# Inverse roots of a graph layer's norms: from GpSimd's power to ScalarE's logarithm and exponential with a Newton step on VectorE

## What is computed

```python
def _layernorm(x, axis=-1, eps=1e-05):
    m, v = jnp.mean(x, axis, keepdims=True), jnp.var(x, axis, keepdims=True)
    return (x - m) / jnp.sqrt(v + eps)

def _L1_gnn_ref(inp, adj, W1, W2, W3):                  # inp = layernorm(x)
    h1, h2, h3 = inp @ W1, inp @ W2, inp @ W3
    e = leaky_relu(einsum('bnd,bmd->bnm', h1, h2), 0.2)
    e = where(adj > 0, e, -1e12)
    return relu(softmax(e) @ h3)

def _L1_ffn_ref(x, Wg, bg, ...):                        # x = layernorm(x)
    top_w, top_i = top_k(x @ Wg + bg, 2)                # then 8 experts, two for each token
```

## Time and profile before

| | us |
|---|---|
| median of 3 runs | 1431.46 (1427.86 to 1432.95) |
| the profiled execution, its own time | 1429.35 |
| its span, first to last instruction | 1427.3 |
| second graph layer, about | 870 to 1132 |
| busy: TensorE, VectorE, ScalarE, GpSimd | 1154.3, 991.3, 694.0, 868.2 |

### The profile page before, as it was taken

One profiled execution on the slowest core, in us unless ns is written; L12 is line 12 of the kernel. 1 busy time (PEld: TensorE's weight loads), 2 busy tenths in 40 slices (PEclk: granted clock), 3 DMA queues, 4 the chain that ended last, 5 costly groups with the idle time before them and its releaser, 6 DMA issues. The chain is left out here.

```text
span 1427.3 us, 33176 instructions
## 1 busy us (share of the span) xinstructions
PE 1154.3 (81%) x9205; PEld 957.5 (67%) x9205; DVE 991.3 (69%) x3903; ACT 694.0 (49%) x1789; POOL 868.2 (61%) x754
## 2 busy tenths in 40 slices
PE   6999999667677741999999993787774199999996
PEld 4776666556676641888888882454543199989995
DVE  4999999978787744577767664878775345565555
ACT  5766666457877831333333331333332145455553
POOL 3567676554477676344444441267777568887887
PEclk9999999899999975999999997777676599999999
DMA  6400000000011112566565673244332245555554
GB/s 186 68 2 2 1 2 2 1 1 24 22 37 41 35 49 79 180 198 199 189 203 192 193 220 108 67 139 121 99 116 63 81 57 72 69 66 67 74 67 46
DMA packets 126253, 122.61 MB, mean 86 GB/s; under 512 B 16576, under 2 KB 108096, under 8 KB 126128
## 3 DMA queue, kind: packets, MB, share of 16 engines
q1 hardware_dynamic: 92720, 85.65, 21.4%
q0 software_dynamic: 32960, 35.36, 12.7%
q10 hardware_dynamic: 448, 0.10, 0.0%
HBM read 76.71 MB, written 44.34 MB: 85 GB/s over the span
## 5 line engine op out<-in xcount | busy, mean ns | idle before, releaser
L2851 POOL DMA_INDIRECT out<-m_yb,m_dsti x142 | 227.5, 1602 | 64.3 <-DVE m_yb L2951 27.4
L2151 POOL DMA_INDIRECT rows<-m_yb,m_dsti x135 | 129.2, 957 | 170.1 <-DVE m_dsti L2282 148.5
L2227 ACT ACTIVATE m_sg<-psum 128x256 f32<-128x256 f32 (+3 forms) x216 | 79.6, 369 | 179.5 <-PE psum L2180 175.5
L1375 POOL DMA_INDIRECT dispatch<-g_flat,g1r_pos x128 | 129.5, 1012 | 51.6 <-issue 32.7
L1117 POOL DMA_INDIRECT dispatch<-common_v,a1r_pos x128 | 125.0, 976 | 52.9 <-issue 35.7
L2180 PE MATMUL psum<-m_xT,m_w 128*128 128x256 f32 (+3 forms) x648 | 140.3, 366 | 0.6 <-ACT m_xT L2218 0.6
L2924 ACT ACTIVATE m_hT<-psum,m_w 128x256 f32<-128x256 f32 (+1 forms) x240 | 92.6, 446 | 98.6 <-PE psum L2878 97.7
L2180 PEld LDWEIGHTS psum<-m_xT,m_w 128*128 128x128 f32 (+1 forms) x648 | 106.2, 178 | 18.3 <-ACT m_xT L2218 1.0
L2889 PE MATMUL psum<-m_w,m_hT 128*128 128x128 f32 x848 | 104.8, 275 | 1.1 <-ACT m_hT L2924 0.6
L2878 PE MATMUL psum<-m_xT,m_w 128*128 128x256 f32 (+1 forms) x480 | 104.0, 360 | 1.0 <-issue 0.8
L2889 PEld LDWEIGHTS psum<-m_w,m_hT 128*128 128x128 f32 x848 | 99.4, 192 | 1.8 <-ACT m_hT L2924 1.6
(11 more groups left out here) (313 smaller groups left out, 3068.7 us busy)
## 6 DMA issues: line engine op xcount, KB each, us to landing
m_w<-in_c_wall SPq DMA_DIRECT2D x54, 533.0 KB
ahead_w<-in_c_wall SPq DMA_DIRECT2D x18, 533.0 KB, 3.5
g1c_y<-rows SPq DMA_DIRECT2D x32, 256.0 KB, 3.4
m_xg<-dispatch SPq DMA_DIRECT2D x47, 132.0 KB
m_xg<-dispatch SPq DMA_DIRECT2D x46, 130.0 KB, 2.2
resident<-in_c_wall SPq DMA_DIRECT2D x8, 578.0 KB, 6.1
out<-x SPq DMA_DIRECT2D x16, 256.0 KB
out<-m_yb,m_dsti POOLq DMA_INDIRECT x142, 3.3
```

Of the source, the lines that this page charges most:

```text
L1375: pool.indirect_dma_start(out=dest, out_offset=bass.IndirectOffsetOnAxis(ap=self.pos[t % 3][:, k, p:p + 1], axis=0), in_=flat[:, p, :], in ...
L2151: pool.indirect_dma_start(out=rows_out, out_offset=bass.IndirectOffsetOnAxis(ap=dsti[j][:, t:t + 1], axis=0), in_=yb[j][:, t, :], in_offse ...
L2227: act.activation(sg[j % 2][0:cn, k, 0:rows], up_banks[j % 2][k][0:cn, 0:rows], ACT.Silu)\
L2851: pool.indirect_dma_start(out=out_rows, out_offset=bass.IndirectOffsetOnAxis(ap=dsti[j][:, t:t + 1], axis=0), in_=yb[j][:, t, :], in_offse ...
```

## The change

Each root is now formed as exp(-0.5 ln v), by two ACTIVATEs on ScalarE (`guess_root`), and mended by one Newton step r = g (1.5 - 0.5 v g^2), three instructions on VectorE (`root`). An Ln on one column stands ahead of ScalarE's loop. GpSimd's loop is left with the scatters: all of a batch at once, in the step in which its positions are due. The diff, with what is only declarations and signals cut:

```diff
                     act.activation(fT[:, :], bT[:, :], ACT.Copy).then_inc(fT_ready.sem, 1)
 
+                def guess_root(i, k):
+                    if not runs(i):
+                        return
+                    act.wait_ge(*vs[k].now(i))
+                    act.wait_ge(*rs_ready[k].before(i))
+                    act.activation(lv[:, k, :], ve[:, k, :], ACT.Ln).then_inc(ln_ready[k].sem, 1)
+                    act.wait_ge(*ln_ready[k].now(i))
+                    act.activation(guess[:, k, :], lv[:, k, :], ACT.Exp, scale=-0.5).then_inc(guessed[k].sem, 1)
+
+                act.activation(ahead.probe[:, :], h3[:, 0, C:C + 1], ACT.Ln)
+
                 def step(g, b, h):
                     flat_T(g - 1)
                     probs_T(g)
                     mixed_out(g)
                     head_xT(g + 1)
+                    guess_root(g, 1)
                     head(g + 1)
+                    guess_root(g + 2, 0)
                     scores_own(g + 1)
...
+                def root(i, k):
+                    if not runs(i):
+                        return
+                    dve.wait_ge(*guessed[k].now(i))
+                    dve.wait_ge(*(flat_ready if k else xn_ready).before(i))
+                    dve.tensor_tensor(square[:, k, :], guess[:, k, :], guess[:, k, :], ALU.mult).then_inc(newton[k].sem, 1)
+                    dve.wait_ge(*newton[k].now(i, 0))
+                    dve.scalar_tensor_tensor(out=miss[:, k, :], in0=square[:, k, :], scalar=-0.5, in1=ve[:, k, :],
+                                             op0=ALU.mult, op1=ALU.mult).then_inc(newton[k].sem, 1)
+                    dve.wait_ge(*newton[k].now(i, 1))
+                    dve.scalar_tensor_tensor(out=rs[:, k, :], in0=miss[:, k, :], scalar=1.5, in1=guess[:, k, :],
+                                             op0=ALU.add, op1=ALU.mult).then_inc(rs_ready[k].sem, 1)
 
                 def head_xn(i):
                     if not runs(i):
                         return
-                    dve.wait_ge(*rs0_ready.now(i))
+                    dve.wait_ge(*rs_ready[0].now(i))
...
                     if t is not None:
                         R.vector_rows(dve, t, bR)
+                    root(g + 1, 0)
                     head_xn(g + 1)
...
                         R.vector_choose(dve, t, bR)
+                    root(g, 1)
                     flat_norm(g, h)
...
-                    pool.tensor_tensor(rs[:, 0, :], ve[:, 0, :], half[:, 0:PG], ALU.pow).then_inc(rs0_ready.sem, 1)
...
-                    pool.tensor_tensor(rs[:, 1, :], ve[:, 1, :], half[:, 0:PG], ALU.pow).then_inc(rs1_ready.sem, 1)
...
                 def step(g, b, h):
-                    t, u, v = [batch_due(g, lag) for lag in (3, 4, 5)]
-                    last = t is not None and BATCHES[t][1] == PG
-                    if v != LAST_PAIR:
-                        some(v, 13, 16)
-                    some(t, 0, 3)
-                    some(u, 5, 11)
-                    root_flat(g)
-                    some(t, 3, 4)
-                    some(u, 11, 12)
-                    root_head(g + 2)
-                    some(t, 4, 5)
-                    some(u, 12, 13 if u != LAST_PAIR else 16)
-                    if last:
-                        R.pool_scatter(pool, t, 0, 2 * PG, batch_rows(flat, t), dest)
+                    t = batch_due(g, 3)
+                    if t is not None:
+                        R.pool_scatter(pool, t, 0, 2 * BATCHES[t][1], batch_rows(flat, t), dest)
```

More of the change, by code:

```diff
@@ L2363, in phase_gnn1 @@
         ve, rs = sb("ve", [128, 2, PG]), sb("rs", [128, 2, PG])
+        lv, guess = sb("lv", [128, 2, PG]), sb("guess", [128, 2, PG])
+        square, miss = sb("square", [128, 2, PG]), sb("miss", [128, 2, PG])
         xn = sb("xn", [128, PG, C])
@@ L2390, in phase_gnn1 @@
         gate = sig("gate")
-        dve_signals = bn + part + vs + [xn_ready, e_steps, rc_ready, x3_ready, flat_ready]\
+        newton, rs_ready = [sig("newton0", 2), sig("newton1", 2)], [sig("rs0_ready"), sig("rs1_ready")]
+        dve_signals = bn + part + vs + newton + rs_ready + [xn_ready, e_steps, rc_ready, x3_ready, flat_ready]\
             + R.dve_signals + M.dve_signals
@@ L2394, in phase_gnn1 @@
         own_ready = sig("own_ready")
-        act_signals = [xT_ready, h12_ready, h3_ready, own_ready, pt_ready, o_ready, fT_ready] + R.act_signals
-        rs0_ready, rs1_ready = sig("rs0_ready"), sig("rs1_ready")
-        pool_signals = [rs0_ready, rs1_ready] + R.pool_signals
+        ln_ready, guessed = [sig("ln0"), sig("ln1")], [sig("guessed0"), sig("guessed1")]
+        act_signals = ln_ready + guessed + [xT_ready, h12_ready, h3_ready, own_ready, pt_ready, o_ready, fT_ready] + R.act_signals
+        pool_signals = R.pool_signals
         pe_xT, pe_h, pe_e, pe_pt, pe_o, pe_fT = sig("pe_xT"), sig("pe_h", 3), sig("pe_e"), sig("pe_pt"), sig("pe_o", 2), sig("pe_fT")
@@ L2603, in head_stats @@
                     norm_stats(dve, lambda p: xt(i, p), st[:, 0, :, :], mv0[i % 2], ve[:, 0, :], bn[0], part[0],
-                               vs[0], i, EPS_LN, gate, [M.mixed.now(i, 1), rs0_ready.before(i)])
+                               vs[0], i, EPS_LN, gate, [M.mixed.now(i, 1), rs_ready[0].before(i)])
+                def root(i, k):
[10 more added lines that the diff above has]
+                                             op0=ALU.add, op1=ALU.mult).then_inc(rs_ready[k].sem, 1)
                 def head_xn(i):
@@ L2649, in flat_stats @@
                     norm_stats(dve, lambda p: xt(i, p), st[:, 1, :, :], mv1, ve[:, 1, :], bn[1], part[1],
-                               vs[1], i, EPS_LN, gate, [x3_ready.now(i), rs1_ready.before(i)])
+                               vs[1], i, EPS_LN, gate, [x3_ready.now(i), rs_ready[1].before(i)])
                 def flat_norm(i, t):
@@ L2654, in flat_norm @@
                         return
-                    dve.wait_ge(*rs1_ready.now(i))
+                    dve.wait_ge(*rs_ready[1].now(i))
                     R.wait_block(dve, i // 2 - 3)
@@ L2683, in _ @@
             def _(pool):
[L2684 to L2688, removed]
-                    pool.tensor_tensor(rs[:, 0, :], ve[:, 0, :], half[:, 0:PG], ALU.pow).then_inc(rs0_ready.sem, 1)
[L2691 to L2695, removed]
-                    pool.tensor_tensor(rs[:, 1, :], ve[:, 1, :], half[:, 0:PG], ALU.pow).then_inc(rs1_ready.sem, 1)
-                def some(t, first, last):
-                    if t is not None and BATCHES[t][1] == PB:
-                        R.pool_scatter(pool, t, first, last, batch_rows(flat, t), dest)
-                def step(g, b, h):
-                    t, u, v = [batch_due(g, lag) for lag in (3, 4, 5)]
-                    last = t is not None and BATCHES[t][1] == PG
-                    if v != LAST_PAIR:
-                        some(v, 13, 16)
-                    some(t, 0, 3)
-                    some(u, 5, 11)
-                    root_flat(g)
-                    some(t, 3, 4)
-                    some(u, 11, 12)
-                    root_head(g + 2)
-                    some(t, 4, 5)
-                    some(u, 12, 13 if u != LAST_PAIR else 16)
-                    if last:
-                        R.pool_scatter(pool, t, 0, 2 * PG, batch_rows(flat, t), dest)
+                def step(g, b, h):
+                    t = batch_due(g, 3)
+                    if t is not None:
+                        R.pool_scatter(pool, t, 0, 2 * BATCHES[t][1], batch_rows(flat, t), dest)
                 in_pairs(step)
```

## The result

The changed kernel takes 1441.41 us (median of 9 runs, 1435.21 to 1442.57), beside 1430.58 for the kernel before (9 runs, 1423.31 to 1432.95). The ratio is 1.0083, with a 95% interval of 1.0066 to 1.0100: slower by 0.8%, some 12 us (the medians lie 10.8 apart). The profiled execution took 1441.74 us; its span is 1439.9. The prediction was 1440.

The account below looks back on a forecast made before the run. VectorE was taken to bound choosing groups, a chain through TensorE and ScalarE rows groups, with GpSimd's lateness hurting a few. Longer groups and start, less a shorter tail, gave +8.4 us on the layer: 1440, range 1435 to 1452.

Parts of the forecast that it names:

- two table loads a root: On ScalarE Ln and Exp each need a table load, four a group, 64 in the layer; chance 0.77.
- The price of a load: On ScalarE a table load costs 1.28 us and nothing beside it, starting as soon as ScalarE is free.
- No drain: ScalarE's trace shows no 1.38 us drain per switch; the rival of a hidden drain gave about 1495 us, chance 0.02.
- X to `scores_own`: From X, the end of `head_xT`, to the start of `scores_own` on ScalarE: about 8.0 us, 1.2 later than before.
- The groups: S(0) to S(15), first to last `soft`: 209.4 us instead of 193.9; choosing groups (with expert choice) 13.8, rows groups 14.35.
- The start: Up to S(0), the first `soft`: the first root adds 1.3 us and loads holding `scores_own` 2.0, together 3.3.
- The tail: After S(15), the last `soft`: `flat_norm` at +10.2 us, positions 9.3 later, then SP's stores, L1498 at +39.4.
- What ends last: Before load L1498: SP's chain, at 1140.1, takes over from GpSimd's, at 1137.8; GpSimd last again would be a wrong sign.
- The layer: At the layer's end, load L1498 comes at 1140.1 against 1131.74, +8.4 us.
- The rival of one table set: On ScalarE one set serves Ln and Exp, a single load: 1423.5 us, between 1419 and 1430; chance 0.18.
- the Newton step: VectorE's three 4-column operations per root: 0.2 us each, 0.6 a root, +0.6 in choosing groups, about +0.4 in rows groups.
- GpSimd's relief: 32 roots, 33 us, leave GpSimd's queue; worst group falls from 15.6 to some 13 us, last `flat_norm` 6.7 us sooner.

Follow-up runs that it names:

- two-load kernel: The changed kernel with both Ln of a step ahead of both Exp, two table loads a group instead of four; 1443.23 us, ratio 1.0090.
- one-set kernel: The changed kernel with the set holding logarithm and exponential loaded by name ahead of ScalarE's loop, instead of an Ln; 1429.95 us, ratio 0.9992.

## Why the prediction was right, and where it was not

The working held because its one large decision did: two table loads a root, 64 in the layer.

- *The price of a load.* 1283 ns each, gaps of 0.02 us, as read from the earlier trace rows. No drain: the Trainium skill's 2.66 us per switch (ScalarE: Activation LUTs, What ACT_TABLE_LOAD costs) isn't seen in these traces, neither at 1011.24 nor in the three back-to-back loads behind it.
- *X to `scores_own`.* Predicted 8.0, measured 7.8 in the choosing group shown and 8.06 (997.83 to 1005.89) in the rows group before it.
- *The groups.* Predicted 209.4 in all, measured 210.2. The choosing groups 4, 6, 8, 10, 12 took 13.54 to 14.07 (predicted 13.8), the rows groups 3, 5, 7, 9, 11 took 14.28 to 14.62 (14.35), group 14 13.19 (13.1).
- *The start.* S(0) is 6.1 later; 2.7 of it lie ahead of the layer, the remaining 3.4 meet the 3.3.
- *The tail.* `flat_norm` at S(15) + 10.1 (predicted 10.2), SP's first store at S(15) + 20.1 (20.45).
- *What ends last.* This step failed, by little. SP's stores should have taken over from GpSimd, 2.3 us behind it. SP's chain was right: last store issued at 1141.38, plus the landing of 2.1 makes 1143.5. But GpSimd needed 62.7 us, not 60.5, for its last 48 scatters (1079.74 to 1142.42), because single ones took up to 1.28 us and one, at 1123.25, stood 1.53 us behind the one before it instead of 0.30, with no wait shown; and it began 0.9 us behind its positions. It stayed last, with L1498 at 1144.05, which the prediction had named among its signs of being wrong; the time hardly shows it, because the two chains end within 0.6 us of each other. In the two-load kernel SP does come last: L1498 stands 3.9 us behind the last scatter there (1143.20, 1147.07).
- *The layer.* +9.6 against a predicted +8.4: 0.8 from the groups, 0.4 behind S(15), 0.1 from the start.
- *The level.* 1440 and 1441.41 lie closer than the changes do. The forecast change was 8.5 us, on a median before of 1431.46 (3 runs); measured are 10.8 by the medians and 12 by the ratio, on 1430.58 (9 runs). Part of the nearness is luck.

The rival of one table set was priced wrong. It was to give 1423.5 and gave 1430. The term that failed is the Newton step: the sum put it at 0.6 us a group, 9 us in the 15, and between S(0) and S(15) it is 15.8 (184.0 to 199.8). Its three operations cost what was said; what the sum left out is that with them more rows groups run at the low clock. A rows group was to take 12.8 and took 13.6 in the mean. A smaller miss lies behind S(15): L1498 was to follow by 39.4 us, behind SP's stores, and follows by 42.3 (1092.52 to 1134.83), 2.6 behind the last scatter, because GpSimd comes last there too. The term opposite, GpSimd's relief, was read from VectorE's waits and from the longest groups; its source is the length of GpSimd's queue, and it is 15.7 us. In parts of the whole: loads +13.0, Newton steps +14.6, relief -15.7, together +11.9 us, the measured 0.83%. Each part is the difference of two neighbouring kernels, so that the parts add up is no check of them.

In the Trainium skill (ScalarE: Activation LUTs, Table sets) Ln then Exp are one load, by a set with both. That set exists, and the one-set kernel runs on it with a single load; but putting an Ln first doesn't select it. The traces disagree with the Trainium skill for a kernel that doesn't name the set.

Open: why more rows groups fall under the low clock when 0.6 us are added. The rows show that they do and what it costs, not what decides it. Whether the loads could all be put where ScalarE waits anyway, and so cost nothing, was not tried.

## What to carry to other kernels

Where two ScalarE functions alternate, count the ACT_TABLE_LOAD rows of the trace, and name a set that holds both rather than hope that the first function brings it: one line was worth 13 us here. Price an operation by the chain that it is put in: 0.16 us instructions on VectorE ate nearly the whole relief of an engine with a full queue (14.6 of 15.7 us), and merging them (8 columns instead of two times 4) or leaving those out that stood ahead of `head_xn` gave back 5 to 6 us. Compare a group with one of the same granted clock before a difference is put down to the instructions in it: here the clock was worth 1.9 us a group and the instructions 0.6. A full queue at the end of a phase costs its own time even when nobody waits for it on the way.

## What was not expected of the hardware

Work on TensorE that nobody reads made a kernel faster: from 890 to 1090 us its granted clock rose from 0.72 to 0.80, and the ratio to before fell from 0.9991 to 0.9948. The granted clock is a mix of the two levels, 1.2 and 2.4 GHz; the same sixteen 128-column products took 1.85 us in a group at 0.63 and 1.09 us in one at 0.85. In two other kernels the same filler raised the clock and changed no time beyond the intervals. In the kernel before VectorE still waited for GpSimd; for the one without the Newton step the reason isn't shown.
